# Second attention: three PSUM banks in one ring for transposes and query lifts, and ACT's bank copies one step later

## The chip, the cores and the metric

The kernel runs on one NeuronCore of a Trainium2 chip. The metric is the device time of one execution in microseconds (us). TensorE is called PE here, VectorE DVE, ScalarE ACT, GpSimd POOL and SyncE SP; PEld is PE's weight load.

## The reference

Two transformer layers over x of 2 x 1024 x 256 in fp32, each with attention and a feed-forward part beside it. The change touches the attention of the second layer alone, a latent attention with 16 heads:

```
q      = rmsnorm(x @ wq_a.T, q_a_ln_w) @ wq_b.T          # q_nope (128) and q_pe (64) per head
ckv    = x @ wkv_a.T                                     # 64 latent + 64 rotary columns
kv     = rmsnorm(ckv[..., :64], kv_a_ln_w)
q_abs  = einsum('bhsd,hdc->bhsc', q_nope, q_absorb)      # 64 per head
scores = (einsum('bhsc,btc->bhst', q_abs, kv) + einsum('bhsd,bxtd->bhst', rope(q_pe), rope(k_pe))) * SCALE
attn   = softmax(where(causal, scores, min))
x      = einsum('bhst,btc->bhsc', attn, kv)              # then out_absorb and wo
```

## The kernel before

The kernel goes through the first layer (until about 665 us), the second attention (`attend1`) and the output product (from 1298 us). All of `attend1` is written out by hand: each engine has its own program, and semaphores tie them together.

**Groups, steps, units.** There are 16 groups of two heads, 8 for each half of the batch. A group has 16 steps; step t takes 128 queries of one head against (i+1) blocks of 128 keys, with i = 0,1,0,1 in steps 0 to 3, then 2,3,2,3, then 4,5,4,5, then 6,7,6,7. Two groups make one iteration of a loop (`n`, with t from 0 to 31). In this text steps count 0 to 15 within a group.

For a step, PE writes the scores into PSUM (`score_pe`, three products for each 512 keys; two buffers of two banks each take turns). DVE finds the row minimum (`softmax_dve`: where i is 4 or more a reduction at L919, then always the masked one at L924). ACT makes the exponential (`softmax_act`, L971) into one of 8 buffers `p`. DVE takes the reciprocal of the sum (L930), POOL scales the rows (L988). Four steps later (LAG = 4) PE transposes the scaled rows, block by block (`turn_pe`, L1027), into a PSUM bank. Up to four blocks in one bank are a **unit**: a step has one unit where i is below 4, else two. So a group has units 0 to 23: unit t for steps 0 to 7, and units 8,9 for step 8 up to 22,23 for step 15. Even units are copied out of PSUM by DVE (L957), odd ones by ACT (L955), into `pt` (`evacuate`). When four steps (both heads, 256 queries) are turned, PE multiplies them with the values two to four steps later (`value_pe`, L1054), and ACT copies the product out (`softmax_out`, L1068).

**The slots.** Each engine's program goes slot by slot. In slot t PE issues: scores of step t, a piece of value products, in slots 0, 2, 4 and 6 one **lift** (a product of 128 x 512 that makes the next group's queries, `prep_pe`, L194), and last the transposes of step t-4. So slot 15 turns step 11 (units 14, 15), and slot 0 of the next group turns step 12 (units 16, 17), behind lift 0. The scores of step t wait until the exponential of step t-2 is done, since they write its buffer.

In slot t ACT issues: the output copy if there is one, the copy of the odd unit that is turned in this same slot t, the exponential of step t, and a piece of the next group's preparation (`prep_act`: L2123 copies lifts 0 and 1 out, L2129 rounds lifts 2 and 3, L2134 rounds the rotated halves in slots 12 and 13). DVE issues in slot t: the copy of the even unit turned in slot t-1, the minimum of step t, the reciprocal of step t-1, and a preparation piece (`prep_dve`: L2143 in slots 5 and 7, L2149 in slots 13 and 14). In slot 15 DVE copies a second unit, the one turned in slot 15 itself, between the reduction and the masked minimum of step 15; slot 0 has no copy on DVE.

**Banks.** Eight PSUM banks: 0 to 3 for scores, 4 and 5 for units (even and odd), 6 for the value product, 7 for the lifts. So unit U waits, before its first transpose, until unit U-2 has been copied out; a lift waits until the lift before it has been read.

Of the kernel before, what the change touches and what calls it, by code (L numbers as in the profile page):

```python
# [4 lines left out]
F32 = mybir.dt.float32  # L5
# [3 lines left out]
ACT = mybir.ActivationFunctionType  # L9
AX = mybir.AxisListType  # L10

P = 128
# [179 lines left out]
def accumulate(e, out, products):  # L192
    for n, (a, b) in enumerate(products):
        ins = e.matmul(out, a, b, start=n == 0, stop=n == len(products) - 1)  # L194
    return ins
# [636 lines left out]
class Core:  # L832
# [3 lines left out]
    def __init__(self, heads, groups):  # L836
        self.heads, self.groups = heads, groups
        self.steps = [(c, hd, 2 * c + i) for c in range(NQC) for hd in range(heads) for i in range(2)]
        self.SG = len(self.steps)
        self.SI = 2 * self.SG  # L840
        self.per_chunk = 2 * heads
        self.pieces = self.per_chunk - 1
        self.out_lag = LAG + 2 + self.pieces
        self.units = [self.n_units(i) for _, _, i in self.steps]
        self.UG = sum(self.units)

    def wide(self, t):

# [84 lines left out]
def evacuate(e, C, s, n, t, later, parity):  # L933

    core = s.core
    tt = t - LAG
    if (tt < 0 and not later) or tt >= core.SI:
        return

    c, hd, i = core.steps[tt % core.SG]  # L940
    u0 = core.unit0(tt % core.SI) + (0 if tt >= 0 else -2 * core.UG)
    mine = s.ev_act if parity else s.ev_dve
    cc = tt // core.SG * NQC + c
    for w in range(core.n_units(i)):
        if (u0 + w) % 2 != parity:
            continue
        U = n * 2 * core.UG + u0 + w
        e.wait_ge(s.turned, U + 1)
        if later or cc >= 2:
            e.wait_ge(s.pv, n * 2 * NQC + cc - 1)  # L950
        k0, k1 = 4 * w, min(4 * w + 4, i + 1)
        dst = s.pt[:, c % 2, hd, k0:k1, (i % 2) * P:(i % 2 + 1) * P]
        src = C.turn[parity][:, 0:(k1 - k0) * P].rearrange("p (k q) -> p k q", q=P)
        if parity:
            e.activation(dst, src, ACT.Copy).then_inc(mine, 1)  # L955
        else:
            e.tensor_copy(dst, src).then_inc(mine, 1)  # L957


def softmax_act(e, C, s, n, t, later):  # L960

    core = s.core
    S = n * core.SI + t
    evacuate(e, C, s, n, t, later, 1)
    if t < core.SI:
        c, hd, i = core.steps[t % core.SG]
        k = t % NST
        e.wait_ge(s.maxed, S + 1)
        if later or t >= NPB:
            e.wait_ge(s.turned, turned_after(core, n, t - NPB))  # L970
        e.activation(s.p[:, t % NPB, 0:(i + 1) * P], C.score[t % 2][:, 0:(i + 1) * P], ACT.Exp,  # L971
                     scale=-1.0, bias=s.nm[:, k:k + 1], accum_out=s.l[:, k:k + 1]).then_inc(s.exped, 1)
# [34 lines left out]
        ins.then_inc(s.scored, 1)  # L1007


def turn_pe(e, C, s, n, t, later):  # L1010

    core = s.core
    S = n * core.SI + t
    if t >= LAG or later:
        tt = t - LAG
        if tt < core.SI:
            c, hd, i = core.steps[tt % core.SG]
            e.wait_ge(s.normed, S - LAG + 1)
            u0 = core.unit0(tt % core.SI) + (0 if tt >= 0 else -2 * core.UG)
            for w in range(core.n_units(i)):  # L1020
                U = n * 2 * core.UG + u0 + w
                par = (u0 + w) % 2
                if later or u0 + w >= 2:
                    e.wait_ge(s.ev_act if par else s.ev_dve, n * core.UG + (u0 + w) // 2)
                k0, k1 = 4 * w, min(4 * w + 4, i + 1)
                for k in range(k0, k1):
                    ins = e.transpose(C.turn[par][:, (k - k0) * P:(k - k0 + 1) * P],  # L1027
                                      s.p[:, tt % NPB, k * P:(k + 1) * P], C.ident[:, :])
                ins.then_inc(s.turned, 1)

# [128 lines left out]
def wait(e, sem, value):  # L1159
    if value > 0:  # L1160
        e.wait_ge(sem, value)
# [907 lines left out]
def attend1(nc, C, W, w_p, wf_d, rows_cos, rows_sin, ql, q_first, keys, v, ot_d):  # L2069
# [3 lines left out]
    with Phase(nc, "a1") as ph:  # L2073
# [17 lines left out]
        qlo = ph.sem("qlo")  # L2091


        def prep_pe(e, g, u, k):
            done = g - 1
            if k == 0:
                e.wait_ge(wf_in[u], wf_count(g, u))
                wait(e, qlo, done * 6)
            elif k <= 2:
                e.wait_ge(raw_out, done * 2 + k)  # L2100
            else:
                e.wait_ge(qhi, done * 6 + 2)
                e.wait_ge(qlo, done * 6 + 2)
            c = k % 2
            m = slice(P, 2 * P) if k < 2 else slice(0, P)
            t = slice(c * HALF, (c + 1) * HALF)
            ql_h, ql_l = ql[g // NG1]
            accumulate(e, C.prep[:, :], [
                (wf[u][:, a, m], x[:, kt, t])
                for a, kt, x in ((0, 0, ql_h), (0, 0, ql_l), (1, 0, ql_h), (2, 1, ql_h), (2, 1, ql_l))]).then_inc(lifted, 1)  # L2110

# [3 lines left out]
        def prep_act(e, g, u, k):  # L2115
            done = g - 1
            if k < 2:
                e.wait_ge(lifted, done * 4 + k + 1)
                if k == 0:
                    wait(e, qhi, done * 6)  # L2120
                    wait(e, qlo, done * 6)
                t = slice(k * HALF, (k + 1) * HALF)
                e.activation(raw[:, t], C.prep[:, :], ACT.Copy).then_inc(raw_out, 1)  # L2123
            elif k < 4:
                e.wait_ge(lifted, done * 4 + k + 1)
                t = slice((k - 2) * HALF, (k - 1) * HALF)
                for hd in range(2):
                    r = LAT_ROWS[hd]
                    e.activation(q[u][hd][0][r, t], C.prep[r, :], ACT.Copy).then_inc(qhi, 1)  # L2129
            else:  # L2130
                hd = k - 4
                r = PE_ROWS[hd]
                e.wait_ge(roped, done * 6 + 6)
                e.activation(q[u][hd][0][r, :], raw[r, :], ACT.Copy).then_inc(qhi, 1)  # L2134

        def prep_dve(e, g, u, k):
            done = g - 1
            if k < 4:
                e.wait_ge(qhi, done * 6 + 2 * (k - 1))
                t = slice((k - 2) * HALF, (k - 1) * HALF)  # L2140
                for hd in range(2):
                    r = LAT_ROWS[hd]
                    e.tensor_tensor(q[u][hd][1][r, t], C.prep[r, :], q[u][hd][0][r, t].bitcast(F32),  # L2143
                                    ALU.subtract).then_inc(qlo, 1)
            else:
                hd = k - 4
                r = PE_ROWS[hd]
                e.wait_ge(qhi, done * 6 + 5 + hd)
                e.tensor_tensor(q[u][hd][1][r, :], raw[r, :], q[u][hd][0][r, :].bitcast(F32),  # L2149
                                ALU.subtract).then_inc(qlo, 1)  # L2150
# [20 lines left out]
        def next_pair(n, t, last, at):  # L2171

            if t >= core.SI or t % PREP not in at or (last and t >= PREP):
                return None
            g = t // PREP
            return n * 2 + g + 1, (g + 1) % 2, at[t % PREP]

        with nc.Block(no_gpsimd_drain=True) as block:

# [33 lines left out]
            @block.tensor  # L2213
            def _(e):
                def score(g, hd, i, k0, k1):
                    q_h, q_l = q[g % 2][hd]
                    kh, kl = keys[g // NG1][hd]
                    a = slice(i * P, (i + 1) * P)
                    return [(q_h[:, a], kh[:, k0:k1]), (q_l[:, a], kh[:, k0:k1]), (q_h[:, a], kl[:, k0:k1])]

                def value(g, hd, k):
                    return v[g // NG1][:, k, :]

                def slot(n, t, later, last):
                    if t < core.SI and t % PREP == 0:
                        g = t // PREP
                        wait(e, qhi, (n * 2 + g) * 6)
                        wait(e, qlo, (n * 2 + g) * 6)
                    score_pe(e, C, s, n, t, later, score)
                    value_pe(e, C, s, n, t, later, value, KL)  # L2230
                    nxt = next_pair(n, t, last, AT_PE)
                    if nxt:
                        prep_pe(e, *nxt)
                    turn_pe(e, C, s, n, t, later)

                core.iterate(e, slot, core.out_lag + 1)

# [96 lines left out]
def program(nc, x, Wq, Wk, Wv, Wp, bp, Wfc, Wproj, wq_a, q_ln, wq_b, wkv_a, kv_ln, wkv_b, wo, w1, w2, w3,  # L2334
# [9 lines left out]
    with ExitStack() as ctx:  # L2344
# [4 lines left out]
        psum = ctx.enter_context(nc.psum_tensor("psum", [P, 8, HALF], F32))  # L2349
        C.banks = [psum[:, i, :] for i in range(8)]  # L2350
        C.score = [psum[:, 2 * i:2 * i + 2, :].rearrange("p a c -> p (a c)") for i in range(2)]
        C.turn = [C.banks[4], C.banks[5]]
        C.prep = C.banks[7]
        C.out = [C.banks[6]]
        C.ident, C.ones = sb("ident", [P, P]), sb("ones", [P, P])
        C.mask_a = sb("mask_a", [P, HALF])
# [101 lines left out]
```

## Time and profile before

| | us |
|---|---|
| three runs | 1360.22, 1364.55, 1370.68 |
| their median | 1364.55 |
| profiled execution, device time | 1362.34 |
| its span in the trace | 1360.5 |
| second attention, from the first scores to the first output product | 665 to 1298 |
| one group in the middle, 14 times the same | 38.57 |

The profile comes from one execution. A timeline row gives the start (us from the span's start), the duration, the engine, the line and the operation; what stands in brackets is how long the engine had been idle and which engine's instruction ended the wait. Rows of neighbouring instructions of one kind are merged (x6). The end of a matmul is modelled and overlaps the next one, so distances on PE are best taken from start to start. Groups 1 to 14 repeat in the trace to within 0.02 us, so one of them is read in detail here (the one whose slot 0 begins at 1008.6 us, with the slot 0 after it at 1047.2 us).

### The profile page before, as it was taken

The numbers are of one execution on the slowest core, as the hardware profiler recorded it, in microseconds if no ns is written. First come the engines' busy times: TensorE is split into PE (matmuls) and PEld (weight loads), VectorE is DVE, ScalarE is ACT, GpSimd is POOL, SyncE is SP. The second block draws the span as 40 slices with busy tenths as digits, with TensorE's granted clock in tenths as the row PEclk, the third lists the DMA queues.
The fourth block names the chain that finished last, engine by engine and source line by source line (L and its number), as shares of the span: only waits on it lengthen the run. The fifth ranks groups of instructions, "written<-read, shape, count | busy, mean of one in ns | idle before, by whom it ended". The sixth has DMA issues, their size and how long they took to land. (4 is left out here: it accounts for less than half of the span.)

```text
span 1360.5 us, 22133 instructions
## 1 busy us (share of the span) xinstructions
PE 1206.2 (89%) x7424; PEld 856.5 (63%) x7424; DVE 881.9 (65%) x2299; ACT 729.0 (54%) x1681; POOL 543.3 (40%) x567
## 2 busy tenths in 40 slices
PE   4897749999999889887699999999999999999788
PEld 3776624444443477776577777767776777776577
DVE  7867359889997345444577776666767766666401
ACT  2565205677776425445566666566666665565400
POOL 2434133444441100616155655544556555545200
PEclk9998857899998797898899999999999999999989
DMA  6760084455540284021300111111101111100091
GB/s 197 142 130 32 32 108 58 57 78 79 69 67 3 67 230 143 22 83 47 101 18 26 44 44 43 44 43 29 32 31 41 43 44 44 44 19 14 32 332 40
DMA packets 112433, 93.53 MB, mean 69 GB/s; under 512 B 49664, under 2 KB 102208, under 8 KB 110528
## 3 DMA queue, kind: packets, MB, share of 16 engines
q1 hardware_dynamic: 112320, 92.11, 29.2%
q8 instruction: 60, 0.98, 0.3%
q14 instruction: 53, 0.43, 0.1%
HBM read 53.02 MB, written 30.67 MB: 62 GB/s over the span
## 5 line engine op out<-in xcount | busy, mean ns | idle before, releaser
L988 POOL TENSOR_SCALAR a_p<-a_p,a_rl 128x128 f32<-128x128 f32 (+7 forms) x256 | 215.7, 844 | 307.7 <-DVE a_rl L930 307.6
L971 ACT ACTIVATE a_p<-psum,a_nm 128x128 f32<-128x128 f32 (+7 forms) x256 | 189.5, 740 | 57.1 <-DVE a_nm L924 55.4
L1485 ACT ACTIVATE a_pt<-psum 128x512 f32<-128x512 f32 (+3 forms) x384 | 167.8, 492 | 78.9 <-PE psum L1345 76.2
L1027 PE MATMUL psum<-ident,a_p 128*128 128x128 f32 x1152 | 175.6, 279 | 13.8 <-DVE a_pt L957 13.8
L957 DVE COPY a_pt<-psum 128x512 f32<-128x512 f32 (+1 forms) x192 | 114.5, 596 | 101.4 <-PE psum L1027 100.6
L955 ACT ACTIVATE a_pt<-psum 128x256 f32<-128x256 f32 (+2 forms) x192 | 87.4, 455 | 156.5 <-PE psum L1027 156.5
L1027 PEld LDWEIGHTS psum<-ident,a_p 128*128 128x128 f32 x1152 | 127.1, 140 | 62.8 <-issue 48.1
L1054 PE MATMUL psum<-a_pt,v 128*64 128x256 f32 (+1 forms) x1280 | 159.4, 370 | 2.3 <-ACT a_ot L1068 2.3
L1335 PE MATMUL psum<-a_op_k,a_op_q 64*128 64x512 f32 (+3 forms) x384 | 135.0, 448 | 23.8 <-DVE a_op_k L1451 22.8
L1345 PE MATMUL psum<-a_op_q,a_op_k 64*128 64x512 f32 (+3 forms) x384 | 129.8, 423 | 8.1 <-ACT a_pt L1485 6.7
L1345 PEld LDWEIGHTS psum<-a_op_q,a_op_k 64*128 64x128 f32 x384 | 63.6, 196 | 104.7 <-ACT a_pt L1485 86.5
L1054 PEld LDWEIGHTS psum<-a_pt,v 128*64 128x64 f32 x1280 | 78.3, 136 | 58.9 <-issue 15.4
L919 DVE TENSOR_REDUCE a_part<-psum 128x1 f32<-128x512 f32 x128 | 87.9, 687 | 33.0 <-PE psum L1006 31.9
L1281 POOL TENSOR_SCALAR_AFFINE_SELECT a_pt<-a_pt 128x512 f32<-128x512 f32 x64 | 41.6, 652 | 127.6 <-ACT a_pt L1485 127.6
L1335 PEld LDWEIGHTS psum<-a_op_k,a_op_q 64*128 64x128 f32 x384 | 69.7, 203 | 35.0 <-issue 23.0
L1366 PE MATMUL psum<-a_pt,a_v 128*32 128x512 f32 (+3 forms) x768 | 89.4, 539 | 2.6 <-ACT a_oraw L1502 1.2
L924 DVE CUSTOM_DVE_ANT_0 psum<-psum,mask_a 128x128 f32<-128x128 f32 (+3 forms) x128 | 63.5, 496 | 30.7 <-PE psum L1006 30.1
L1421 DVE TENSOR_REDUCE a_part<-psum 128x1 f32<-128x512 f32 x128 | 82.3, 680 | 0.0
L924 DVE CUSTOM_DVE_ANT_0 psum<-psum,mask_a,a_part 128x128 f32<-128x128 f32 (+3 forms) x128 | 71.4, 558 | 3.9
L1427 DVE CUSTOM_DVE_ANT_0 psum<-psum,mask_a,a_part 128x128 f32<-128x128 f32 (+3 forms) x128 | 66.2, 554 | 8.3 <-PE psum L1335 8.1
L194 PE MATMUL psum<-w_of,o_ot 128*128 128x256 f32 x256 | 58.6, 394 | 10.0 <-DMA o_x<-acc_d 10.0
L1427 DVE CUSTOM_DVE_ANT_0 psum<-psum,mask_a 128x128 f32<-128x128 f32 (+3 forms) x128 | 59.1, 520 | 11.7 <-PE psum L1335 11.3
(355 smaller groups left out, 2770.8 us busy)
## 6 DMA issues: line engine op xcount, KB each, us to landing
ot_d<-a_ot SPq DMA_DIRECT2D x16, 512.0 KB, 2.8
o_ot<-ot_d SPq DMA_DIRECT2D x8, 1024.0 KB, 9.5
a_swap<-w_p SPq DMA_DIRECT2D x60, 128.0 KB, 2.3
a_raw_q<-qk_d SPq DMA_DIRECT2D x48, 128.0 KB, 4.7
room<-qk_d SPq DMA_DIRECT2D x48, 128.0 KB, 7.8
w<-wf_d SPq DMA_DIRECT2D x15, 384.0 KB, 3.4
qk_d<-d_stage_h SPq DMA_DIRECT2D x64, 64.0 KB, 2.1
qk_d<-d_stage_l SPq DMA_DIRECT2D x64, 64.0 KB, 2.1
```

Of the source, the lines that this page charges most:

```text
L919: e.tensor_reduce(so_far, C.score[t % 2][:, 0:k0], AX.X, ALU.min).then_inc(s.halved, 1)
L924: e.tensor_tensor_reduce(out=tail, in0=tail, in1=C.mask_a[:, HALF - (k1 - k0):HALF], scale=1.0, scalar=so_far, op0=ALU.add, op1=ALU.min, a ...
L957: e.tensor_copy(dst, src).then_inc(mine, 1)
L971: e.activation(s.p[:, t % NPB, 0:(i + 1) * P], C.score[t % 2][:, 0:(i + 1) * P], ACT.Exp, scale=-1.0, bias=s.nm[:, k:k + 1], accum_out=s.l ...
L988: e.tensor_scalar(s.p[:, t % NPB, 0:(i + 1) * P], s.p[:, t % NPB, 0:(i + 1) * P], s.rl[:, k:k + 1], 1.0, ALU.mult, ALU.mult).then_inc(s.no ...
L1027: ins = e.transpose(C.turn[par][:, (k - k0) * P:(k - k0 + 1) * P], s.p[:, tt % NPB, k * P:(k + 1) * P], C.ident[:, :])
L1054: ins = e.matmul(out[width * hd:width * (hd + 1), q0:QC], value(2 * n + g, hd, k), s.pt[:, c % 2, hd, k, q0:QC], start=k == 0, stop=k == n ...
L1335: e.matmul(bank_a("score", g, k)[:, 0:k1 - k0], q[rows(hd), hd % 2, i * P:(i + 1) * P], kk[rows(hd), hd % 2, k0:k1], start=True, stop=True ...
L1345: e.matmul(bank_b("score", g, k)[:, off:HALF], kk[rows(hd), hd % 2, j * P:(j + 1) * P], q[rows(hd), hd % 2, c * HALF + off:(c + 1) * HALF] ...
L1366: ins = e.matmul(pv_bank[32 * hd:32 * (hd + 1), off:HALF], v[g % 3][:, hd, j, :], pt[:, u % NPT, hd, off:HALF], start=j == 0, stop=j == 4 ...
L1427: e.tensor_tensor_reduce(out=bank[:, 0:n], in0=bank[:, 0:n], in1=C.mask_a[:, HALF - n:HALF], scale=1.0, scalar=so_far, op0=ALU.add, op1=AL ...
L1485: e.activation(pt[:, k // G0 % NPT, hd, off:HALF], bank_b("score", g, k)[:, off:HALF], ACT.Exp, scale=-1.0).then_inc(exped, 1)
```

## The change

The private banks are given up. Banks 4, 5 and 7 form one ring, and its users, units and lifts alike, take the banks in turn in the order in which PE issues them (`Core.share`). A user waits until the user three places before it has been read: a unit until it is copied, lift 0 or 1 until ACT has copied it (`raw_out`), lift 2 or 3 until ACT and DVE have both read it (`qhi`, `qlo`). The order from slot 15 on is: units 14, 15 | lift 0, units 16, 17 | 18, 19 | lift 1, 20, 21 | 22, 23 | lift 2, unit 0 | 1 | lift 3, 2 | 3 | 4 | 5 | 6 | 7 | 8, 9 | 10, 11 | 12, 13 (the bars part the slots). In the last group there are no lifts.

The other part: in slot t ACT copies the odd unit turned in slot t-1, not in slot t, before the exponential of step t. DVE's program stays as it was.

```diff
+    def share(self, banks, lift_of):
+        order = []
+        for n in range(self.groups // 2):
+            for t in range(self.SI):
+                lift = lift_of(n, t)
+                if lift:
+                    order.append(("lift", *lift))
+                tt = n * self.SI + t - LAG
+                if tt >= 0:
+                    order += self.units_of(tt)
...
+        for r, user in enumerate(order):
+            self.at[user] = banks[r % len(banks)]
+            self.held[user] = order[r - len(banks)] if r >= len(banks) else None
...
 def softmax_act(e, C, s, n, t, later):
-    evacuate(e, C, s, n, t, later, 1)
+    evacuate(e, C, s, n, t - 1, later, 1)
...
 def turn_pe(...)
-                par = (u0 + w) % 2
-                if later or u0 + w >= 2:
-                    e.wait_ge(s.ev_act if par else s.ev_dve, n * core.UG + (u0 + w) // 2)
+                free(e, ("unit", U))
+                bank = core.at["unit", U]
...
+        def free(e, user):
+            old = core.held[user]
+            if old and old[0] == "unit":
+                e.wait_ge(s.ev_act if old[1] % 2 else s.ev_dve, old[1] // 2 + 1)
+            elif old:
+                _, g, u, k = old
+                if k < 2:
+                    e.wait_ge(raw_out, (g - 1) * 2 + k + 1)
+                else:
+                    e.wait_ge(qhi, (g - 1) * 6 + 2 * (k - 1))
+                    e.wait_ge(qlo, (g - 1) * 6 + 2 * (k - 1))
+
         def prep_pe(e, g, u, k):
-            done = g - 1
             if k == 0:
                 e.wait_ge(wf_in[u], wf_count(g, u))
-                wait(e, qlo, done * 6)
-            elif k <= 2:
-                e.wait_ge(raw_out, done * 2 + k)
-            else:
-                e.wait_ge(qhi, done * 6 + 2)
-                e.wait_ge(qlo, done * 6 + 2)
+            free(e, ("lift", g, u, k))
...
-        C.turn = [C.banks[4], C.banks[5]]
-        C.prep = C.banks[7]
+        C.ring = [C.banks[4], C.banks[5], C.banks[7]]
```

PE, DVE, POOL and SP issue the same rows in the same order as before. ACT's order moves in two ways that matter. The first place is the border between two groups, from ACT's exponential of step 12 (128x896) to that of step 1 of the next group (128x256). In it `a1_pt` is a copied unit, `a1_p` an exponential, `a1_ot` the output copy; 2x128 is unit 15 and 3x128 unit 17. Before:

```order
L971 ACTIVATE a1_p,a1_l<-psum,a1_nm 128x896
L955 ACTIVATE a1_pt<-psum 128x2x128
L971 ACTIVATE a1_p,a1_l<-psum,a1_nm 128x1024
L1068 ACTIVATE a1_ot<-psum 128x256
L955 ACTIVATE a1_pt<-psum 128x3x128
L971 ACTIVATE a1_p,a1_l<-psum,a1_nm 128x128
L2123 ACTIVATE w_p<-psum 128x512
```

and in the changed kernel:

```order
L995 ACTIVATE a1_p,a1_l<-psum,a1_nm 128x896
L979 ACTIVATE a1_pt<-psum 128x128
L995 ACTIVATE a1_p,a1_l<-psum,a1_nm 128x1024
L1091 ACTIVATE a1_ot<-psum 128x256
L979 ACTIVATE a1_pt<-psum 128x2x128
L995 ACTIVATE a1_p,a1_l<-psum,a1_nm 128x128
L2152 ACTIVATE w_p<-psum 128x512
```

Here the first row is the exponential of step 14, the 128x1024 one that of step 15. Unit 15's copy stood before the exponential of step 15 and now stands behind it and behind the output copy; unit 13's copy (128x128) has come before that exponential in its place.

The second place is ACT in slots 7 to 10, where the copies are of units 3 (2x128) and 5 (4x128). Before:

```order
L955 ACTIVATE a_pt<-psum 128x2x128
L971 ACTIVATE a_p,a_l<-psum,a_nm 128x512
L1068 ACTIVATE a_ot<-psum 128x256
L971 ACTIVATE a_p,a_l<-psum,a_nm 128x640
L955 ACTIVATE a_pt<-psum 128x4x128
L971 ACTIVATE a_p,a_l<-psum,a_nm 128x768
```

and in the changed kernel:

```order
L995 ACTIVATE a_p,a_l<-psum,a_nm 128x512
L1091 ACTIVATE a_ot<-psum 128x256
L979 ACTIVATE a_pt<-psum 128x2x128
L995 ACTIVATE a_p,a_l<-psum,a_nm 128x640
L995 ACTIVATE a_p,a_l<-psum,a_nm 128x768
L979 ACTIVATE a_pt<-psum 128x4x128
```

The exponential of step 7 (128x512) no longer has a copy of a unit turned in its own slot before it; the copy stands before the exponential of step 8, and unit 5's moves behind that of step 9.

## Rows read from the trace of the kernel before

**Rows 1.** The profile's page: the span, and PE's busy time.

```profile
span 1360.5 us, 22133 instructions
...
PE 1206.2 (89%) x7424; PEld 856.5 (63%) x7424; DVE 881.9 (65%) x2299; ACT 729.0 (54%) x1681; POOL 543.3 (40%) x567
```

**Rows 2.** Table by windows, 700 to 1240: PE, PEld, DVE, ACT, POOL; clock, DMA.

```profile
700.00:1240.00 540.00, 522.99 (x3418) 384.70 (x3417) 376.15 (x1036) 335.52 (x784) 294.33 (x308) 1.00 0.13 38
```

**Rows 3.** Waits of PE, 704 to 1243: us in total, times, longest.

```profile
PE psum L1027 <- DVE a_pt L957: 12.2, 15, 0.8
PE psum L1006 <- ACT a_p L971: 4.4, 14, 0.9
```

**Rows 4.** Timeline of DVE, slots 13 to 15: start, us, instruction, idle before.

```profile
1041.45 1.22 DVE L2149 TENSOR_TENSOR q00l<-w_p,q00h 64x1024 fp32r<-64x1024 f32 x1
...
1045.77 0.68 DVE L957 COPY a_pt<-psum 128x512 f32<-128x512 f32 x1
1046.37 0.68 DVE L919 TENSOR_REDUCE a_part<-psum 128x1 f32<-128x512 f32 x1
1047.26 0.69 DVE L957 COPY a_pt<-psum 128x512 f32<-128x512 f32 x1 [0.21 <-PE psum L1027]
```

**Rows 5.** Timeline of PE, from slot 15 to slot 1.

```profile
1045.13 0.39 PE L1006 MATMUL psum<-k11h,w_lat 128*128 128x512 f32 x1
1045.35 0.40 PE L1006 MATMUL psum<-k11l,w 128*128 128x512 f32 x1
1046.59 0.84 PE L1027 MATMUL psum<-ident,a_p 128*128 128x128 f32 x6 [0.85 <-DVE a_pt L957]
1047.19 0.30 PE L1006 MATMUL psum<-k10h,q00h 128*128 128x128 f32 x1
...
1048.77 0.93 PE L1027 MATMUL psum<-ident,a_p 128*128 128x128 f32 x7
1049.96 0.39 PE L1006 MATMUL psum<-k10h,q00h 128*128 128x256 f32 x1 [0.27 <-ACT a_p L971]
```

**Rows 6.** Timeline of ACT, slots 15 and 0.

```profile
1047.47 0.39 ACT L955 ACTIVATE a_pt<-psum 128x256 f32<-128x256 f32 x1 [1.63 <-PE psum L1027]
1048.71 1.11 ACT L971 ACTIVATE a_p<-psum,a_nm 128x1024 f32<-128x1024 f32 x1 [0.85 <-DVE a_nm L924]
...
1050.08 0.49 ACT L955 ACTIVATE a_pt<-psum 128x384 f32<-128x384 f32 x1
```

**Rows 7.** Timelines of DVE, PE and ACT around slot 8, in a middle group.

```profile
1029.52 0.69 DVE L2143 TENSOR_TENSOR q01l<-psum,q01h 64x512 fp32r<-64x512 f32 x1
...
1030.09 0.52 PE L1027 MATMUL psum<-ident,a_p 128*128 128x128 f32 x3
1030.40 0.73 PE L1006 MATMUL psum<-k10h,w 128*128 128x512 f32 x2
...
1030.15 0.20 ACT L971 ACTIVATION_READ_ACCUMULATOR a_p<-psum,a_nm 128x1 f32 x1
```

**Rows 8.** The same place in the first group.

```profile
682.60 0.69 DVE L2143 TENSOR_TENSOR w_lat<-psum,w 64x512 fp32r<-64x512 f32 x1
...
682.21 0.52 PE L1027 MATMUL psum<-ident,a_p 128*128 128x128 f32 x3
```

**Rows 9.** Timelines around slots 11 and 13: DVE, ACT, PE.

```profile
1035.80 0.69 DVE L919 TENSOR_REDUCE a_part<-psum 128x1 f32<-128x512 f32 x1 [0.29 <-PE psum L1006]
...
1037.12 0.90 ACT L971 ACTIVATE a_p<-psum,a_nm 128x768 f32<-128x768 f32 x1 [0.28 <-DVE a_nm L924]
...
1038.16 0.72 PE L1006 MATMUL psum<-k10h,w 128*128 128x512 f32 x2
```

**Rows 10.** Timelines of ACT and PE, slots 3 to 5 of the last group.

```profile
1249.93 0.60 ACT L955 ACTIVATE a_pt<-psum 128x512 f32<-128x512 f32 x1 [1.34 <-PE psum L1027]
...
1250.34 0.30 PE L1027 MATMUL psum<-ident,a_p 128*128 128x128 f32 x1
1251.04 0.72 PE L1006 MATMUL psum<-k10h,w 128*128 128x512 f32 x2 [0.40 <-ACT a_p L971]
```

More of the change, by code:

```diff
@@ L845, in __init__, with units_of @@
         self.UG = sum(self.units)
+        self.at, self.held = {}, {}
+    def share(self, banks, lift_of):
[8 more added lines that the diff above has]
+                    order += self.units_of(tt)
+        for tt in range(n * self.SI + self.SI - LAG, (n + 1) * self.SI):
+            order += self.units_of(tt)
+        for r, user in enumerate(order):
+            self.at[user] = banks[r % len(banks)]
+            self.held[user] = order[r - len(banks)] if r >= len(banks) else None
+    def units_of(self, step):
+        U = step // self.SI * 2 * self.UG + self.unit0(step % self.SI)
+        return [("unit", U + w) for w in range(self.units[step % self.SG])]
     def wide(self, t):
@@ L952, in evacuate @@
         dst = s.pt[:, c % 2, hd, k0:k1, (i % 2) * P:(i % 2 + 1) * P]
-        src = C.turn[parity][:, 0:(k1 - k0) * P].rearrange("p (k q) -> p k q", q=P)
+        src = bank[:, 0:(k1 - k0) * P].rearrange("p (k q) -> p k q", q=P)
         if parity:
@@ L1007, in score_pe, with turn_pe @@
         ins.then_inc(s.scored, 1)
-def turn_pe(e, C, s, n, t, later):
+def turn_pe(e, C, s, n, t, later, free):
     core = s.core
@@ L1021, in turn_pe @@
                 U = n * 2 * core.UG + u0 + w
-                par = (u0 + w) % 2
-                if later or u0 + w >= 2:
-                    e.wait_ge(s.ev_act if par else s.ev_dve, n * core.UG + (u0 + w) // 2)
+                free(e, ("unit", U))
+                bank = core.at["unit", U]
                 k0, k1 = 4 * w, min(4 * w + 4, i + 1)
                 for k in range(k0, k1):
-                    ins = e.transpose(C.turn[par][:, (k - k0) * P:(k - k0 + 1) * P],
+                    ins = e.transpose(bank[:, (k - k0) * P:(k - k0 + 1) * P],
                                       s.p[:, tt % NPB, k * P:(k + 1) * P], C.ident[:, :])
@@ L2107, in prep_pe @@
             ql_h, ql_l = ql[g // NG1]
-            accumulate(e, C.prep[:, :], [
+            accumulate(e, core.at["lift", g, u, k][:, :], [
                 (wf[u][:, a, m], x[:, kt, t])
@@ L2122, in prep_act @@
                 t = slice(k * HALF, (k + 1) * HALF)
-                e.activation(raw[:, t], C.prep[:, :], ACT.Copy).then_inc(raw_out, 1)
+                e.activation(raw[:, t], core.at["lift", g, u, k][:, :], ACT.Copy).then_inc(raw_out, 1)
             elif k < 4:
@@ L2128, in prep_act @@
                     r = LAT_ROWS[hd]
-                    e.activation(q[u][hd][0][r, t], C.prep[r, :], ACT.Copy).then_inc(qhi, 1)
+                    e.activation(q[u][hd][0][r, t], core.at["lift", g, u, k][r, :], ACT.Copy).then_inc(qhi, 1)
             else:
@@ L2142, in prep_dve @@
                     r = LAT_ROWS[hd]
-                    e.tensor_tensor(q[u][hd][1][r, t], C.prep[r, :], q[u][hd][0][r, t].bitcast(F32),
+                    e.tensor_tensor(q[u][hd][1][r, t], core.at["lift", g, u, k][r, :], q[u][hd][0][r, t].bitcast(F32),
                                     ALU.subtract).then_inc(qlo, 1)
@@ L2176, in next_pair @@
             return n * 2 + g + 1, (g + 1) % 2, at[t % PREP]
+        core.share(C.ring, lambda n, t: next_pair(n, t, n == NG // 2 - 1, AT_PE))
         with nc.Block(no_gpsimd_drain=True) as block:
@@ L2233, in slot @@
                         prep_pe(e, *nxt)
-                    turn_pe(e, C, s, n, t, later)
+                    turn_pe(e, C, s, n, t, later, free)
                 core.iterate(e, slot, core.out_lag + 1)
```

## The prediction, made before the changed kernel ran

> **What bounds the kernel now.** I read the page first: the span is 1360.5 us and PE is busy for 89% of it [rows 1]. The profiled execution took 1362.34 us, 1.84 more than its span and 2.2 less than the median of the three runs shown, 1364.55. The changed stage is the second attention. The table by windows gives PE 97% busy there, against 70% for DVE and 62% for ACT, at a granted clock of 1.00, which is 2.4 GHz [rows 2]. Since ends of matmuls are modelled, that busy share doesn't say how much PE waits, so I went on to the waits and then to the timeline of one group, taking PE from start to start.
>
> The waits show PE held twice in each group: 15 times by a DVE copy before transposes, 14 times by an exponential before scores [rows 3]. In the timeline the first is in slot 15: the last score product starts at 1045.35, and unit 14's transposes start at 1046.59 [rows 5]. From one product of 512 columns to the next it is 0.22 us (1045.13 to 1045.35), so 1.02 us of the 1.24 are a wait [rows 5]. It ended 0.14 us after the end of DVE's copy of unit 12 (1045.77 + 0.68 = 1046.45) [rows 4, 5]. The second is at the scores of step 1. The seven transposes from 1048.77 on are those of units 16 and 17; six of them in a row take 0.60 us until the next product (1046.59 to 1047.19), so seven take 0.70, and the scores could have started at 1049.47. They started at 1049.96, when the exponential of step 15 was done: 0.49 us are a wait [rows 5].
>
> Why are these two late? Both hang on DVE. From 1041.45 to the end of step 15's minimum its queue holds a subtraction of 1.22 us, a copy, a reduction and a minimum, a second such subtraction, the copy of unit 12, the reduction of step 15, the copy of unit 14 and the minimum. The one idle time that the timeline reports in it is 0.21 us before unit 14's copy, ended by PE [rows 4]. Step 15's exponential starts as soon as this chain is through: ACT had been idle for 0.85 us and DVE ended the wait [rows 6]. So at the border of two groups DVE's queue sets the time. From score 1 on to slot 8, PE has no wait in the timeline and its own work sets the pace.
>
> **The bubble in slot 15.** Unit 14 now asks for unit 11's copy (ACT, in slot 14) and not for unit 12's. It starts at once, near 1045.6. Unit 15 takes over the wait for unit 12's copy and can start at 1046.45 + 0.14 = 1046.59; that is where unit 14 started before. So PE reaches slot 0 about 0.4 us earlier. This is worth nothing by itself, since PE must wait for step 15's exponential anyhow. What it gives to the end is DVE's 0.21 us of idling: unit 14 is ready when DVE has finished its reduction. Two DVE instructions back to back overlap by 0.08 in these rows (1045.77 + 0.68 against 1046.37), so the copy moves from 1047.26 to 1046.37 + 0.68 - 0.08 = 1046.97, and with it the minimum and the exponential of step 15: **-0.29 us**.
>
> **The new wait in slot 0.** Unit 17 is the third user behind unit 15 (15, lift 0, 16, 17), so it needs unit 15's copy, as it did before. But that copy used to stand before the exponential of step 15, at 1047.47, and ended long before unit 17 came. Now ACT makes it after that exponential and after the output copy. From rows of before: behind the exponential that starts at 1048.71, the copy in that place starts at 1050.08, 1.37 us later [rows 6]. Unit 15 has 256 columns, 0.39 us [rows 6], so it ends 1.76 after the exponential's start. Add 0.14 until PE's first transpose (by the DVE copy above, the nearest row; no row shows PE released by an ACT copy, and from the read of an exponential's sum to PE's scores it is 0.05, 1030.15 + 0.20 against 1030.40 [rows 7], so 0.05 to 0.15) and 0.30 for three transposes until the next product (half of the six above). The scores of step 1 then start 2.20 us after the exponential of step 15 starts. Before it was 1049.96 - 1048.71 = 1.25 us [rows 5, 6]. This is **+0.95 us**, and since everything on PE from score 1 to slot 8 follows without slack, it stays in the period. Queued behind the waiting unit 17 are the scores of step 1 and the value products, and behind these DVE's and ACT's next steps.
>
> Sum at a border: +0.66 us. It holds at 14 borders, those where lift 0 stands in slot 0: 14 x 0.66 = **+9.2 us**.
>
> **Unit 4 behind lift 3.** The third user before unit 4 is lift 3, whose bank is free when DVE has made both subtractions of slot 7. The second ends at 1029.52 + 0.69 = 1030.21, and 0.14 later is 1030.35; unit 4's transposes start at 1030.09 now [rows 7]. That is +0.26. Of this up to 0.05 comes back: the scores of step 9 start at 1030.40, 0.05 behind the read of step 7's sum [rows 7], which is the distance of a wait, and that exponential no longer has unit 3's copy before it. +0.21 in each of 14 middle groups, **+2.9 us**. In the first group the subtractions are later: 682.60 + 0.69 + 0.14 = 683.43 against 682.21, 1.22 later [rows 8]. This group begins without a predecessor's transposes and value products, so PE has less to do and more slack there, in which part of it may vanish; I take **+0.5 us**, between 0 and 1.2.
>
> **What comes back from earlier exponentials.** ACT's copies no longer hold an exponential until PE has turned a unit in the same slot. In slots 11 to 13 that could end PE's wait before step 13's scores, but the rows deny it: the reduction starts when PE's scores of step 11 are there, the exponential of step 11 was released by DVE, not by the copy before it, and the scores of step 13 start at 1038.16 after it [rows 9]. This chain has no copy in it: zero. In the last group, without lifts, it does count: the exponential of step 3 stands behind unit 23's copy, which began at 1249.93 when PE had turned it, and the scores of step 5 wait for it until 1251.04, where PE was done with unit 0 at 1250.34 + 0.03 [rows 10]: -0.67. With the -0.29 at its border (unit 17 asks for DVE's copy of unit 14 there) and the 0.05 at step 9 this is **-1.0 us**, once.
>
> All other new waits I priced at nothing, each with its cover: units 5 to 13 and 18 to 23 ask for copies that are one or two slots old; the closest is unit 10 behind unit 7, which ACT now copies in slot 12, a slot before it is asked for. Lift 0 asks for unit 13, copied before the exponential of step 15 in ACT's idle time. If a cover is gone, the price is a copy, at most 0.6 us per group.
>
> Sum: 9.2 + 2.9 + 0.5 - 1.0 = +11.6 us. Against the profiled execution's 1362.34 this is 1373.9, against the median 1376.2. I forecast **1374**. Bounds of the terms: the border between +0.5 (release 0.05) and +0.95 (no credit from DVE), unit 4 between 0 and +0.3, the first group's as given. That is 14 x 0.5 - 1.0 = +6 to 14 x 1.25 + 1.2 - 1.0 = +18 us, 1368 to 1380.
>
> The rule on the other side is in the Trainium skill, page Perfetto Trace Analysis, section Identifying Performance Opportunities: a gap that repeats on the engine that should be saturated can mean that there was no PSUM for the next tile. By that rule a third bank is the cure, and the first rival is what comes of it. The trace agrees that the gap repeats, 15 times at 0.8 us, but DVE's full queue stands behind it.
>
> **Rivals.** *The bank was what lacked.* PE loses both waits, 15 x (1.02 + 0.49) = 22.7 us, and pays unit 4's 2.9: 1342.5. For it: both waits are real, and the first is one for a bank. Against it: the second ends with DVE's chain, in which the third bank saves only 0.21. It would need DVE to finish step 15's minimum 1.5 us earlier. Chance 0.04.
>
> *The copy doesn't hold unit 17.* The border then gains DVE's 0.29 and nothing is lost, if ACT's copy of unit 15 came in time; the unit-4 wait stays: 1362.3 - 15 x 0.29 + 2.9 + 0.5 - 0.7 = 1360.7. This is also about the case in which the change does nothing for the end. Against it: ACT's order shows the copy behind the exponential, and ACT keeps its order. Chance 0.08.
>
> *Slower by more than 1%.* DVE gives no credit: unit 14's transposes, although their bank is free, don't reach DVE before 1047.0, because they now wait for ACT's copy of unit 11, which stands behind a rounding of 1.04 us in slot 13. The border then costs the full 0.95: 14 x 0.95 + 2.9 + 0.5 - 0.7 = +16.0, 1378.3 by the profiled execution and 1380.5 by the median. It decides where unit 11's copy ends after 1046.4; by the timeline ACT is free of it near 1043.9. Other prices at their upper bounds lead to the same place. Chance 0.22.
>
> **How the numbers follow.** The forecast has 0.66. A measurement of this kernel tells about 1% (13.6 us) from no change. The forecast's middle lies within 1%, its upper end above; I give 0.10 of its 0.66 to above. Faster: the first rival, 0.04. Slower: 0.18 of the third rival's 0.22 and 0.10, so 0.28. Same: 0.68. The range takes in the second rival and the third: 1360 to 1382; what is left out is the first rival and larger prices of the third.
>
> **What would show it.** Right: the wait of PE before unit 14 in slot 15 shrinks to nothing, a short one stands before unit 15; a new wait of about 1.5 us of PE, released by ACT's copy, stands before unit 17 in slot 0, 14 times; the scores of step 1 start 2.2 us behind step 15's exponential; PE waits for DVE's subtraction before unit 4; a group takes 39.4 us instead of 38.57; and PE's clock stays at 1.00 through it, as it does with today's gap of 1.24. Wrong: if the group's period stays at 38.6 or falls, then unit 17 found its bank free or DVE's chain got shorter. I would then look first at the end of unit 15's copy and at DVE's rows from 1041 on.

## The result, and the profile after

| | kernel before | changed kernel |
|---|---|---|
| median of 15 runs each, us | 1360.47 | 1370.58 |
| ratio of the runs, 95% interval | | 1.0066 [1.0044, 1.0089] |
| profiled execution, us | 1362.34 | 1374.75 |
| its span | 1360.5 | 1373.0 |

The changed kernel is slower by 0.66%, 9 us; the two medians differ by 10.1. The forecast of 1374 was +11.6 us over the profiled execution's 1362.34; over the median of the three earlier runs, 1364.55, it is +9.5.

First the waits of PE in the middle groups, which answer to [rows 3]. In this view of the changed kernel the columns are the us in total, the times and the longest:

```profile
PE psum L1050 <- ACT a_pt L979: 18.7, 14, 1.3
PE psum L1050 <- DVE a_pt L981: 4.4, 14, 0.3
```

DVE's copy holds PE for 0.3 us at a time where it was 0.8, and scores no longer wait for an exponential. In their place stands one wait of 1.3 us before transposes, 14 times, ended by ACT's copy. PE idled 16.6 us in this list before and idles 23.1 now.

The timeline of PE from slot 15 to slot 1 of a middle group, in answer to [rows 5]:

```profile
1053.79 0.39 PE L1030 MATMUL psum<-k11l,w 128*128 128x512 f32 x1
1054.02 0.60 PE L1050 MATMUL psum<-ident,a_p 128*128 128x128 f32 x4
1054.93 0.44 PE L1050 MATMUL psum<-ident,a_p 128*128 128x128 f32 x2 [0.32 <-DVE a_pt L981]
1055.13 0.31 PE L1030 MATMUL psum<-k10h,q00h 128*128 128x128 f32 x1
...
1056.71 0.60 PE L1050 MATMUL psum<-ident,a_p 128*128 128x128 f32 x4
1058.64 0.55 PE L1050 MATMUL psum<-ident,a_p 128*128 128x128 f32 x3 [1.34 <-ACT a_pt L979]
1058.94 0.36 PE L1030 MATMUL psum<-k10h,q00h 128*128 128x256 f32 x1
...
1094.45 0.42 PE L1030 MATMUL psum<-k10h,w 128*128 128x128 f32 x2
```

Unit 14 (x4) starts 0.23 behind the last score product, so the bubble is gone. Unit 15 (x2) has a short wait. Unit 16 goes straight on at 1056.71, and unit 17 (x3) stands still until 1058.64. The last row is the slot 0 of the next group: 1094.45 - 1055.13 = 39.32 us, where it was 38.57.

Why unit 17 stands still is in ACT's timeline of the same stretch (compare [rows 6]):

```profile
1056.83 1.11 ACT L995 ACTIVATE a_p<-psum,a_nm 128x1024 f32<-128x1024 f32 x1 [2.39 <-DVE a_nm L947]
1057.85 0.19 ACT L995 ACTIVATION_READ_ACCUMULATOR a_p<-psum,a_nm 128x1 f32 x1
1057.94 0.37 ACT L1091 ACTIVATE a_ot<-psum 128x256 f32<-128x256 f32 x1
1058.20 0.39 ACT L979 ACTIVATE a_pt<-psum 128x256 f32<-128x256 f32 x1
```

ACT was idle for 2.39 us, and PE had turned unit 15 by 1055.37 (1054.93 + 0.44), so the copy could have run in that time; but the exponential stood before it in ACT's order, and that waited for DVE until 1056.83. The copy of unit 15 (128x256) ends at 1058.59; 0.05 later PE goes on. DVE's own stretch has lost its gap:

```profile
1054.20 0.68 DVE L981 COPY a_pt<-psum 128x512 f32<-128x512 f32 x1
1054.81 0.67 DVE L942 TENSOR_REDUCE a_part<-psum 128x1 f32<-128x512 f32 x1
1055.40 0.67 DVE L981 COPY a_pt<-psum 128x512 f32<-128x512 f32 x1
1056.00 0.74 DVE L947 CUSTOM_DVE_ANT_0 psum<-psum,mask_a,a_part 128x512 f32<-128x512 f32 x1
```

From the copy of unit 12 to that of unit 14 it is 1.20 us now and was 1.49 [rows 4]: the credit of 0.29.

Slot 8, DVE and PE, in answer to [rows 7]:

```profile
1037.75 0.69 DVE L2172 TENSOR_TENSOR q01l<-psum,q01h 64x512 fp32r<-64x512 f32 x1
```

```profile
1038.20 0.28 PE L1030 MATMUL psum<-k10l,w 128*128 128x128 f32 x1
1038.59 0.52 PE L1050 MATMUL psum<-ident,a_p 128*128 128x128 f32 x3
1038.86 0.70 PE L1030 MATMUL psum<-k10h,w 128*128 128x512 f32 x2
```

The second subtraction ends at 1038.44 and unit 4 starts 0.15 later. From the product before it to the scores of step 9 it is 0.66 us (1038.20 to 1038.86); before it was 0.43 (1029.97 to 1030.40), with unit 4's transposes following the product without a gap.

Taken slot by slot from the starts of the scores, over the 14 middle groups, slot 15 went from 3.08 to 2.57 us, slot 0 from 2.77 to 3.81, slot 8 from 1.39 to 1.61, slot 1 and slot 9 each lost 0.02. All others are equal to 0.01. That is +0.52 at the border (slots 15, 0 and 1) and +0.21 in slots 8 and 9, +0.73 a group. In the span: 14 x 0.73 = 10.2, the first group +0.56, the last group with the end +0.86, and +0.83 before the second attention, in code that did not change. The sum is 12.5, the difference of the spans.

### The profile page after: what moved, and what is told of

It reads as the page before. It is cut to its first block and busy times, and to the rows that moved or that the text cites. A ratio compares the mean times of both kernels' runs of the same rounds, so it can differ in the third digit from the quotient of the medians.

```text
span 1373.0 us, 22135 instructions
## 1 busy us (share of the span) xinstructions
PE 1210.6 (88%) x7424; PEld 862.6 (63%) x7424; DVE 876.4 (64%) x2299; ACT 733.6 (53%) x1681; POOL 545.1 (40%) x567
## 5 line engine op out<-in xcount | busy, mean ns | idle before, releaser
L1050 PE MATMUL psum<-ident,a_p 128*128 128x128 f32 x1152 | 182.7, 282 | 26.3 <-ACT a_pt L979 18.7
L947 DVE CUSTOM_DVE_ANT_0 psum<-psum,mask_a 128x128 f32<-128x128 f32 (+3 forms) x128 | 63.5, 496 | 40.7 <-PE psum L1030 40.2
L721 POOL TENSOR_TENSOR d_h<-d_r 128x512 f32<-128x512 f32 x32 | 44.1, 1383 | 52.1 <-ACT d_r L663 45.7
```

Source lines behind the costliest of these rows:

```text
L947: e.tensor_tensor_reduce(out=tail, in0=tail, in1=C.mask_a[:, HALF - (k1 - k0):HALF], scale=1.0, scalar=so_far, op0=ALU.add, op1=ALU.min, a ...
L1050: ins = e.transpose(bank[:, (k - k0) * P:(k - k0 + 1) * P], s.p[:, tt % NPB, k * P:(k + 1) * P], C.ident[:, :])
```

## Experiments

Each kernel's ratio is to runs of the kernel before on the same chip, with a 95% interval; the group time is the median over the middle groups of the one profiled execution. The changed kernel ran 15 times, those with six units exchanged and the one with the later copies alone 6 times, the one with short subtractions 4 times, the others 12 times.

| kernel | ratio | group, us |
|---|---|---|
| before | 1 | 38.57 |
| changed | 1.0066 [1.0044, 1.0089] | 39.30 |
| ring alone | 1.0039 [1.0006, 1.0072] | 38.88 |
| later copies alone | 1.0195 [1.0152, 1.0238] | 40.17 |
| changed, unit 15 early | 0.9999 [0.9969, 1.0029] | 38.48 |
| and unit 4's exception | 0.9947 [0.9920, 0.9974] | 38.20 |
| before, copiers exchanged | 0.9954 [0.9925, 0.9983] | 38.17 |
| before, short subtractions | 0.9871 [0.9833, 0.9908] | 37.70 |
| before, exchanged for units 10 to 15 | 0.9842 [0.9814, 0.9870] | 37.47 |
| ring of unit 4's exception, the same exchange | 0.9869 [0.9833, 0.9905] | 37.58 |

### The ring alone

```diff
--- changed kernel
-    evacuate(e, C, s, n, t - 1, later, 1)
+    evacuate(e, C, s, n, t, later, 1)
```

> The ring of three banks alone; ACT copies in the slot in which the unit is turned, as before. Theory A (the loss at the group border comes from ACT's later copy of unit 15, the loss in slot 8 from the ring): at a border DVE's minimum of step 15 comes 0.29 us earlier and nothing waits for unit 15, slot 8 costs 0.21 us. 15 x -0.29 + 14 x 0.21 + 0.5 = about -1 us, ratio 0.999, a middle group 38.5 us. Theory B (the banks shared with the lifts cost the time): as slow as the changed kernel, ratio about 1.007, 39.3 us. Theory C (a bank was what lacked, and ACT's order hides the gain): both waits of PE go, -20 us, ratio 0.985.

Measured: 1.0039, a group 38.88. None of the three theories has that number. The border moved as theory A says (slots 15 and 0 together from 5.85 to 5.54), and slot 8 cost its 0.22. But a wait came up that I had not listed, in the list of PE's waits:

```profile
PE psum L1050 <- ACT w_p L2152: 4.9, 14, 0.4
```

It is unit 22 in slot 3. In the ring it stands third behind lift 1, whose bank ACT frees. ACT's timeline in slot 2, then PE's row of unit 22:

```profile
1061.04 0.49 ACT L979 ACTIVATE a_pt<-psum 128x384 f32<-128x384 f32 x1 [2.38 <-PE psum L1050]
1061.42 0.36 ACT L995 ACTIVATE a_p<-psum,a_nm 128x128 f32<-128x128 f32 x1
1061.67 0.20 ACT L995 ACTIVATION_READ_ACCUMULATOR a_p<-psum,a_nm 128x1 f32 x1
1061.76 0.60 ACT L2152 ACTIVATE w_p<-psum 128x512 f32<-128x512 f32 x1
```

```profile
1062.51 1.06 PE L1050 MATMUL psum<-ident,a_p 128*128 128x128 f32 x8 [0.35 <-ACT w_p L2152]
```

With ACT's copy in the same slot, the copy of lift 1 (`w_p`) is queued behind the copy of unit 21, which waits until PE has turned it, after the lift. In the changed kernel the lift's copy is free to run before that, and the wait isn't there. So the ring by itself costs 0.31 us a group: -0.31 at the border, +0.22 in slot 8, +0.39 in slot 3.

### The later copies alone

```diff
--- kernel before
-    evacuate(e, C, s, n, t, later, 1)
+    evacuate(e, C, s, n, t - 1, later, 1)
```

> ACT's copies one slot later, banks as before. Theory A: unit 17 waits for unit 15's copy behind the exponential of step 15, so the scores of step 1 start 2.1 us behind that exponential's start instead of 1.25: +0.86 us at each of 15 borders, nothing in slot 8, -0.05 at step 9, and -0.7 once in the last group: +11.5 us, ratio 1.0085, a middle group 39.4 us. Theory B: no loss, since no bank is shared: ratio 1.000 or a little below by the earlier exponentials, 38.5 us. Theory C: as B.

Measured: 1.0195, a group 40.17. The direction is theory A's and the size is twice as large. The waits of PE show why:

```profile
PE psum L1027 <- ACT a_pt L955: 27.5, 26, 1.1
PE psum L1027 <- DVE a_pt L957: 11.0, 13, 0.8
```

ACT's copy holds PE 26 times, twice in a group. One is unit 17 (slots 0 and 1 grow by 0.83). The other stands in slot 12; the PE timeline of a middle group, then ACT's:

```profile
1048.18 0.60 PE L1027 MATMUL psum<-ident,a_p 128*128 128x128 f32 x4
1049.75 0.33 PE L1027 MATMUL psum<-ident,a_p 128*128 128x128 f32 x1 [0.97 <-ACT a_pt L955]
```

```profile
1047.95 0.90 ACT L971 ACTIVATE a_p<-psum,a_nm 128x768 f32<-128x768 f32 x1 [1.15 <-DVE a_nm L924]
...
1049.10 0.60 ACT L955 ACTIVATE a_pt<-psum 128x512 f32<-128x512 f32 x1
```

Unit 9 needs unit 7's bank, and unit 7's copy now stands behind the exponential of step 11. In the ring unit 9 asks for unit 6, which DVE copies. So here the third bank does help: it takes away a wait of 0.97 us that the later copies bring, and by which slot 12 grew by 0.85. (The wait before unit 17 is 1.14 us here.) In the profiled execution the last group with the end took 4.4 us more as well (62.81 against 58.38), with the clock at its lower level twice, as told below. The two parts of the change cannot be added up: +0.31 and +1.60 alone, +0.73 together.

### The changed kernel with unit 15 copied early

```diff
--- changed kernel
-    evacuate(e, C, s, n, t - 1, later, 1)
+    if t % core.SG:
+        evacuate(e, C, s, n, t - 1, later, 1)
+    if t % core.SG == core.SG - 1:
+        evacuate(e, C, s, n, t, later, 1)
```

> The changed kernel, except that in slot 15 ACT copies the units of slots 14 and 15, both before the exponential of step 15, and none in slot 0. Theory A: the wait of PE before unit 17 vanishes and the 0.29 us from DVE stay; slot 8 costs 0.21 us as in the changed kernel: 15 x -0.29 + 14 x 0.21 + 0.5 - 0.7 = about -1.6 us against the kernel before, ratio 0.999, a middle group 38.5 us. Theory B: as the changed kernel, 1.007. Theory C: faster by both waits, 0.985.

Measured: 0.9999, a group 38.48, theory A's number. PE no longer stands before unit 17; its seven transposes are in one piece, and the scores wait for the exponential:

```profile
1047.08 0.93 PE L1053 MATMUL psum<-ident,a_p 128*128 128x128 f32 x7
1048.47 0.39 PE L1033 MATMUL psum<-k10h,q00h 128*128 128x256 f32 x1 [0.46 <-ACT a_p L998]
```

The exponential started at 1047.21, so the scores follow by 1.26 us instead of 2.11. This is one copy moved back ahead of the exponential and the output copy, once a group, and it gives back 0.82 us: the loss of the change is this place in ACT's queue. Shown.

### Unit 4's exception

```diff
--- the kernel with unit 15 early: Core.share
-        for r, user in enumerate(order):
-            self.at[user] = banks[r % len(banks)]
-            self.held[user] = order[r - len(banks)] if r >= len(banks) else None
+        line, last = list(range(len(banks))), {}
+        for user in order:
+            b = line.pop(1 if user[0] == "unit" and user[1] % self.UG == 4 else 0)
+            line.append(b)
+            self.at[user], self.held[user] = banks[b], last.get(b)
+            last[b] = user
```

> The kernel with ring, later copies and unit 15 copied early, and one exception in the ring: unit 4 takes the bank of unit 2, unit 5 that of lift 3. Theory A (unit 4's wait for DVE's subtraction is what slot 8 costs): PE's wait before unit 4 goes, 0.21 us per group, group 38.27 us instead of 38.48; -5 us against the kernel before, ratio 0.996. Rival: the 0.21 is taken up by the waits in slots 12 and 13, group 38.48, ratio 0.999.

Measured: 0.9947, a group 38.20; slot 8 is 1.34 us. The wait was worth 0.28 and not 0.21, since with the exponential of step 7 early too, the 0.05 of step 9 goes as well. A bank out of turn is free where the one in turn is not: users of a ring that are freed by different engines don't come free in the order of use.

### Who copies, on the kernel before

```diff
--- kernel before: evacuate, turn_pe (value_pe likewise)
-        if (u0 + w) % 2 != parity:
+        if (u0 + w) % 2 == parity:
...
-        src = C.turn[parity][...]
+        src = C.turn[1 - parity][...]
...
-                    e.wait_ge(s.ev_act if par else s.ev_dve, ...)
+                    e.wait_ge(s.ev_dve if par else s.ev_act, ...)
```

> The kernel before with the copies exchanged: ACT copies the even units (512 columns in two-unit steps), DVE the odd ones (128 to 512 columns). Theory A (DVE's queue in slots 13 to 15 sets the border): DVE copies units 11, 13 and 15 there, 256, 128 and 256 columns at about 0.42, 0.29 and 0.42 us, instead of three of 0.69, so the exponential of step 15 starts 0.9 to 1.1 us earlier and PE's waits in slots 15 and 1 shrink by as much: 15 x -1.0 = -15 us, ratio 0.989, a middle group 37.5 us. Theory C (the bank wait sets it): unit 14 now waits for ACT's copy of unit 12, which is early, so the wait in slot 15 goes, but the wait before step 1 grows by the same; no change. If ACT becomes the bound by its longer copies: slower.

Measured: 0.9954, a group 38.17. Theory A's gain at the border is there in full: slots 15 and 0 together take 4.76 us instead of 5.85, -1.09. Some 0.7 us of it is lost before the scores of step 10, which wait for the exponential of step 8, and this for DVE's minimum. DVE's timeline in slots 7 and 8:

```profile
1025.89 0.68 DVE L2143 TENSOR_TENSOR q00l<-psum,q00h 64x512 fp32r<-64x512 f32 x1 [0.48 <-ACT q01h L2129]
...
1027.33 0.42 DVE L957 COPY a_pt<-psum 128x256 f32<-128x256 f32 x1
1027.67 0.68 DVE L919 TENSOR_REDUCE a_part<-psum 128x1 f32<-128x512 f32 x1
```

DVE idles for 0.48 us before the subtraction because ACT, which now copies unit 2, rounds lift 3 later, and the copy of unit 3 stands on DVE before the reduction of step 8. I had not foreseen it; when I wrote the next round's expectations I took ACT's copy of unit 4 before that exponential for the cause, and this timeline, in which DVE released the exponential, says otherwise.

### Short subtractions on the kernel before

```diff
--- kernel before: prep_dve, k = 4 and 5
-                e.tensor_tensor(q[u][hd][1][r, :], raw[r, :], q[u][hd][0][r, :].bitcast(F32),
+                e.tensor_tensor(q[u][hd][1][r, 0:P], raw[r, 0:P], q[u][hd][0][r, 0:P].bitcast(F32),
                                 ALU.subtract).then_inc(qlo, 1)
```

> The kernel before, its two DVE subtractions of slots 13 and 14 cut to 128 of 1024 columns, so the low halves of the rotated queries are left out but for these. Theory A (DVE's queue sets the border): 2 x 0.9 us of DVE work less before step 15's minimum, of which about 1.0 us reaches the end, since then the reduction of step 15 waits for PE's scores; PE's wait in slot 15 goes though its bank rule is unchanged; group 37.6 us, 15 x -1.0 = -15 us, ratio 0.989. Theory C (the bank wait is a cause of its own): the wait before unit 14 stays at about 1 us.

This kernel leaves out the low halves of the rotated queries in 896 of 1024 columns, so it computes something else and serves only for its times. Measured: 0.9871, a group 37.70. The bank rule is that of the kernel before, and yet the wait before unit 14 is gone. PE's timeline in slot 15, and DVE's:

```profile
1035.82 0.39 PE L1006 MATMUL psum<-k11l,w 128*128 128x512 f32 x1
1036.05 0.82 PE L1027 MATMUL psum<-ident,a_p 128*128 128x128 f32 x6
```

```profile
1034.73 0.28 DVE L2149 TENSOR_TENSOR q01l<-w_p,q01h 64x128 fp32r<-64x128 f32 x1
1034.94 0.68 DVE L957 COPY a_pt<-psum 128x512 f32<-128x512 f32 x1
1036.25 0.69 DVE L919 TENSOR_REDUCE a_part<-psum 128x1 f32<-128x512 f32 x1 [0.63 <-PE psum L1006]
```

The copy of unit 12 is done at 1035.62, before PE asks for its bank, and DVE now waits for PE, as was expected. Two banks are enough when DVE comes in time. Set beside the kernel with unit 15 early, where the third bank took the same bubble away and the border gained 0.31, against 0.88 here, this settles what the bubble meant: DVE's queue, not PSUM.

### Exchanged for six units, without and with the ring

```diff
--- kernel before
+    def copier(self, U):
+        u = U % self.UG
+        return 1 - u % 2 if 10 <= u < 16 else u % 2
...
-        if (u0 + w) % 2 != parity:
+        if core.copier(u0 + w) != parity:
...
-        src = C.turn[parity][...]
+        src = C.turn[(u0 + w) % 2][...]
...
-                    e.wait_ge(s.ev_act if par else s.ev_dve, ...)
+                    e.wait_ge(s.ev_act if core.copier(u0 + w - 2) else s.ev_dve, ...)
```

> The kernel before, with the copiers exchanged for units 10 to 15 alone: DVE copies 11, 13, 15, ACT 10, 12, 14. Theory A: the gain of the full exchange at the border (1.09 us) without its new wait at step 10 (0.7 us, unit 4 copied by ACT before the exponential of step 8): group 37.5 us, 15 x -1.09 = -16 us, ratio 0.988. Rival (the 0.7 comes from ACT's longer copies as such): group 38.2 us as in the full exchange, ratio 0.995.

Measured: 0.9842 [0.9814, 0.9870], a group 37.47. This version beats both kernels. Of the 21.5 us by which its span is shorter, 16.8 lie in the second attention (616.4 us instead of 633.2, near the 16 expected). In its one profiled execution the stage also began earlier, at 660.6 instead of 665.3; over all kernels run that start lies between 658.7 and 667.3, with no change in the code before it, and what moves it stays open. DVE's timeline in slots 14 and 15:

```profile
1029.80 1.20 DVE L2153 TENSOR_TENSOR q01l<-w_p,q01h 64x1024 fp32r<-64x1024 f32 x1
1030.93 0.27 DVE L961 COPY a_pt<-psum 128x128 f32<-128x128 f32 x1
1031.20 0.69 DVE L923 TENSOR_REDUCE a_part<-psum 128x1 f32<-128x512 f32 x1
1031.86 0.42 DVE L961 COPY a_pt<-psum 128x256 f32<-128x256 f32 x1
```

Copies of 0.27 and 0.42 us stand where two of 0.68 stood.

> The ring kernel with unit 15 early and unit 4's exception, and the copiers exchanged for units 10 to 15. In the ring units 13 and 15 then wait for ACT's copies of units 10 and 12, the first behind a rounding of 1.04 us, about 0.3 us late. Theory A: group 37.5 to 37.7 us, -13 to -16 us, ratio 0.989: the third bank adds nothing once DVE's queue is shorter. Theory C (a bank lacks): clearly below the same exchange without the ring, under 37.2 us.

The same `copier` in the ring kernel with both repairs. Measured: 0.9869 [0.9833, 0.9905], a group 37.59. Its interval and that of the kernel without the ring overlap, so the ratios don't rank the two; the group time is 0.11 longer with the ring. That is slot 14, 2.88 us against 2.73, where unit 13 now waits for ACT's copy of unit 10, which stands behind a rounding of 1.04 us, as was expected. ACT's row, then PE's:

```profile
1027.93 0.58 ACT L986 ACTIVATE a_pt<-psum 128x512 f32<-128x512 f32 x1
```

```profile
1027.99 0.91 PE L1060 MATMUL psum<-ident,a_p 128*128 128x128 f32 x5
```

The copy ends at 1028.51, and the five transposes with that wait take 0.66 us until the next scores (1028.65). Without these 0.15 us the ring would be ahead by 0.04. Theory C's 37.2 did not come: once DVE's queue is shorter, the third bank gives next to nothing.

## Why the prediction came out

The direction, the place and nearly the size were right. Step by step:

**The bubble in slot 15.** Right: unit 14 starts at once, unit 15 takes over a short wait, and what reached the end is 0.29 us from DVE. The rival in which a bank was lacking, at 1342.5 us and a chance of 0.04, would have needed both waits to end. The rival with no credit from DVE had a row wrong: in the kernel before, ACT's rounding in slot 13 ends at 1043.18 + 1.04 = 1044.22, not near 1043.9. It doesn't matter; in the changed kernel unit 11's copy ends at 1052.35, 1.67 us before unit 14 asks for its bank. The page of the Trainium skill that stands behind it (Perfetto Trace Analysis, Identifying Performance Opportunities) says that such a gap can mean a lack of PSUM; in this kernel the run with short subtractions shows that it did not.

**The new wait in slot 0.** Right in its cause, a little high in its size. The scores of step 1 follow the exponential's start by 2.11 us (1058.94 - 1056.83), not 2.20. I took the release of PE from a row with a DVE copy, 0.14, and here it is 0.05 (1058.59 to 1058.64), the lower end that I had named. The engine is not what differs: in the changed kernel DVE's copy of unit 12 releases unit 15 in 0.05 too (1054.20 + 0.68 to 1054.93), and with the ring alone ACT's copy of lift 1 releases unit 22 in 0.15 (1061.76 + 0.60 to 1062.51). In the middle groups of these traces a wait for a bank ends 0.14 to 0.15 us before the transposes where the unit is the first of its slot, and 0.05 where it is the second; why is not shown. The border costs +0.52 where I had +0.66, and 0.09 of the difference is this. It is 2 us over 14 borders.

**Unit 4 behind lift 3.** +0.21 as written, and +0.56 in the first group against +0.5.

**Earlier exponentials.** The middle groups gained nothing, as the chain through steps 11 and 13 said: from the last transpose to step 13's scores it stays at 0.37 to 0.38 us in all kernels but those with the later copies alone (0.08) and the full exchange (0.32). **The last group is the step that failed:** I had -1.0 us and the trace has +0.86 with the end of the stage. The gains are there at first: up to the scores of step 15 the last group is 0.59 us ahead of the kernel before. Then two things take it back. The first value product after the last scores now waits for unit 15's copy (0.28 us later than in the kernel with unit 15 early). And from there PE ran at a lower clock, which is told below; from that value product to the first one of the next chunk it took 8.17 us instead of 6.92. In the kernel with unit 15 early, the last group with the end takes 57.39 us against 58.38 before: that is the -1.0.

**All other waits at nothing.** Right for the changed kernel, but more by the pairing of its parts than by my covers. Either part alone has a wait, of 0.35 us (ring) or 0.97 us (later copies), that I had not listed, even when I wrote their expectations. I had looked up each user's place in the ring, and not what stands before its copy in ACT's queue. The list had holes too: it leaves out units 0 to 3 and lifts 1 to 3, and units 18 and 22 stand behind lifts 0 and 1, not behind units. None of them waits in the changed kernel; unit 22 does with the ring alone.

**The two errors** nearly cancel in the sum: -2 us at the borders and +1.9 in the last group. The difference of 11.6 us that I had by the terms is the 11.6 us that the second attention grew by in the profiled executions (633.2 to 644.8); in the medians it is 10.1. That agreement is luck: two terms were off by 2 us each, in opposite directions, and the last group's term is read from one execution of each kernel.

## What to carry over

Before a bank or buffer is added for a gap that repeats, follow the engine that frees it: if its queue is full, the gap moves and the end stays. Here relieving that queue gave 1.1 us a group, and the third bank, with both of its own faults repaired, 0.4. When a copy moves behind another instruction on an in-order engine, the price is not the copy but everything that the instruction before it waits for; check that for each user of the freed buffer, at every place where two loops meet.

## What the runs showed of the hardware

**The clock after a pause of PE.** At the end of the last group PE's granted clock fell in some kernels. In the changed kernel the windows before and at the place are as follows. The columns are the window and its length in us, the busy time of PE, PEld, DVE, ACT and POOL with their instructions (x), the clock, the DMA share and GB/s:

```profile
1285.00:1289.00 4.00, 2.02 (x15) 1.46 (x13) 2.32 (x7) 1.78 (x6) 1.31 (x2) 1.00 0.01 2
1289.00:1293.00 4.00, 3.68 (x18) 2.46 (x20) 1.17 (x2) 0.68 (x3) 1.12 (x1) 0.59 0.00 0
```

and in the kernel before:

```profile
1274.00:1278.00 4.00, 2.01 (x15) 1.46 (x13) 2.31 (x7) 2.22 (x7) 1.33 (x2) 1.00 0.01 2
1278.00:1282.00 4.00, 3.89 (x31) 2.66 (x31) 1.32 (x3) 0.94 (x2) 1.12 (x1) 1.00 0.00 0
```

In the changed kernel PE had stood still before it:

```profile
1286.77 0.55 PE L1050 MATMUL psum<-ident,a_p 128*128 128x128 f32 x3 [0.29 <-DVE a_pt L981]
1289.32 1.67 PE L1077 MATMUL psum<-a_pt,v 128*64 128x256 f32 x8 [2.01 <-ACT a_pt L979]
1290.92 1.97 PE L1050 MATMUL psum<-ident,a_p 128*128 128x128 f32 x8
```

A clock of 0.59 is a stretch mostly at 1.2 GHz. Eight transposes took 1.97 us where they take 1.09 at full clock. The waits before the place were 2.01 us here, after one of 0.29; in the kernel with the later copies alone 0.82 and 1.79, and in the last kernel of the table 1.85: in these three the clock fell, and from the first value product there to that of the next chunk it took 8.16 or 8.17 us, where it took 6.59 in the kernel with unit 15 early. In the kernel with the later copies alone it also fell at the last group's start, behind waits of 0.84, 0.37 and 1.79 us (0.57 from 1264 to 1268). At the place above it did not fall in the seven other kernels, for instance behind 1.28 us (the kernel before, with 0.82 earlier) or behind 1.78 us (the kernels with the ring alone or unit 15 early, with 0.29 earlier). PE was busy for the same 2.0 of 4 us ahead of it in the changed kernel and in the one before. In the middle groups of the changed kernel the clock stayed at 1.00 (700 to 1240 us) through waits of 1.34 us. What decides, and whether it falls in each execution, stays open; there is one profiled execution of each kernel.
